# Cross-attention with MLP: context turned by VectorE from 32x32 blocks, a third buffer for the exponentials, new orders

## What is computed

```python
qn = layer_norm(Q, ln_q_g, ln_q_b)                     # Q: [16, 512, 256]
q = heads(qn @ Wq + bq)                                # 16 heads of 16
k, v = heads(KV @ Wk + bk), heads(KV @ Wv + bv)        # KV: [16, 1601, 256]
attn = softmax(einsum('bhqd,bhkd->bhqk', q, k) / sqrt(16))
ctx = einsum('bhqk,bhkd->bhqd', attn, v)
x = Q + (merge(ctx) @ Wo + bo)
h = layer_norm(x, ln_ff_g, ln_ff_b)
return x + silu(h @ W1 + b1) @ W2 + b2
```

## Time and profile before

| | us |
|---|---|
| median of 3 runs | 3438.5 (3438.05 to 3440.09) |
| the profiled execution | 3438.9 |
| its span, first to last instruction | 3437.1 |

### The profile page before, as it was taken

The page is one execution under the profiler, slowest core; times in us unless marked ns, Lnnn a source line. Parts: engine busy times, 40 slices in busy tenths (PEclk is TensorE's granted clock), DMA queues, the critical chain, the costliest instruction groups (busy, mean ns, idle before and its releaser), DMA issues.

```text
span 3437.1 us, 52453 instructions
## 1 busy us (share of the span) xinstructions
PE 3363.7 (98%) x19620; PEld 1621.4 (47%) x19620; DVE 2505.0 (73%) x4613; ACT 2240.1 (65%) x2859; POOL 952.1 (28%) x1340
## 2 busy tenths in 40 slices
PE   6899999999999999999999999999999999999997
PEld 2334544444444445444445444444444455444435
DVE  5777777777777867777777777767777777777761
ACT  2566667666676666667666676666767666676663
POOL 5032324223332322324222232232314222242201
PEclk7999999999999999999999999999999999999998
DMA  4322212232122322212232122321223231122200
GB/s 103 64 42 44 51 33 55 45 71 42 35 48 36 71 45 43 50 37 57 45 69 38 32 54 38 70 45 35 51 39 61 45 64 36 35 55 43 45 7 13
DMA packets 121534, 162.95 MB, mean 47 GB/s; under 512 B 37040, under 2 KB 102592, under 8 KB 118208
## 3 DMA queue, kind: packets, MB, share of 16 engines
q1 hardware_dynamic: 120896, 159.40, 23.6%
q10 hardware_dynamic: 384, 0.20, 0.0%
HBM read 46.43 MB, written 8.39 MB: 16 GB/s over the span
## 4 chain that ended last, share of the span: by engine, by line
PE 95%; DVE 2%; ACT 1%; SPq 0%; DMA 0%; issue 0%; POOL 0%; ACTq 0%; DVEq 0%
PE o_ps L1241 23%; PE rows_ps L1207 22%; PE scores L1222 21%; PE side L1171 6%; PE side L1175 6%; PE side L1160 5%; PE side L1152 5%; DVE chunk_max L1006 2%; PE side L1156 2%; PE side L1164 2%; PE side L1143 1%; PE side L1146 0%; ACT probs L811 0%; PE scores L1171 0%; PE side L1167 0%; PE side L1150 0%
## 5 line engine op out<-in xcount | busy, mean ns | idle before, releaser
L1006 DVE TENSOR_REDUCE chunk_max<-rows_ps 128x1 f32<-128x512 f32 (+1 forms) x3328 | 2110.8, 666 | 778.7 <-PE rows_ps L1207 772.0
L811 ACT ACTIVATE probs<-scores 128x1024 f32<-128x1024 f32 (+1 forms) x1664 | 1653.4, 1022 | 727.8 <-PE scores L1222 559.7
L1207 PE MATMUL rows_ps<-k_stack,q_stack 96*128 96x512 bf16 (+1 forms) x4096 | 1139.5, 337 | 22.6 <-DVE chunk_max L1006 15.9
L1222 PE MATMUL scores<-q_stack,k_stack 99*128 99x512 bf16 (+1 forms) x3328 | 984.9, 379 | 5.0 <-ACT probs L811 3.0
L1241 PE MATMUL o_ps<-probs,v_sb 128*32 128x512 f32 x6656 | 850.2, 602 | 2.3 <-ACT probs L811 2.2
L1207 PEld LDWEIGHTS rows_ps<-k_stack,q_stack 96*128 96x128 bf16 x4096 | 338.3, 98 | 717.7 <-DVE chunk_max L1006 469.7
L1222 PEld LDWEIGHTS scores<-q_stack,k_stack 99*128 99x128 bf16 (+1 forms) x3328 | 320.0, 99 | 391.1 <-issue 94.5
L1241 PEld LDWEIGHTS o_ps<-probs,v_sb 128*32 128x32 f32 x6656 | 148.9, 108 | 359.8 <-issue 280.9
L648 POOL TENSOR_TENSOR o_sb<-o_sb,denom 128x512 f32<-128x512 f32 x32 | 40.6, 1268 | 896.5 <-DVE denom L992 896.5
L592 POOL TENSOR_TENSOR rest<-whole,k_parts 128x512 f32<-128x512 f32 x124 | 117.1, 944 | 548.7 <-ACT k_parts L776 541.8
L1175 PE MATMUL side<-w_sb,ffT 128*128 128x256 f32 x960 | 261.3, 381 | 0.0
(11 more groups left out here) (130 smaller groups left out, 2160.0 us busy)
## 6 DMA issues: line engine op xcount, KB each, us to landing
k_stack<-k_parts SPq DMA_DIRECT2D x768, 50.0 KB, 2.2
k_stack<-k_stack SPq DMA_DIRECT2D x192, 200.1 KB, 5.6
ctx_nat<-in_ctx SPq DMA_DIRECT2D x47, 512.0 KB, 4.0
q_stack<-q_stack SPq DMA_DIRECT2D x192, 64.0 KB, 3.4
q_stack<-q_parts SPq DMA_DIRECT2D x756, 16.0 KB, 1.8
x_nat<-in_x SPq DMA_DIRECT2D x16, 512.0 KB, 6.0
resid<-in_x SPq DMA_DIRECT2D x32, 256.0 KB, 2.8
out<-resid SPq DMA_DIRECT2D x32, 256.0 KB, 2.4
```

The source lines that it names most:

```text
L811: nc.scalar.activation(probs[0:rows, (q + t) % 2, 2 * LQ * pair:2 * LQ * (pair + 1)], scores[0:rows, 2 * LQ * pair:2 * LQ * (pair + 1)], A ...
L1006: nc.vector.tensor_reduce(dst, src, AX.X, ALU.max).then_inc(rows_read, 1)
L1207: last = nc.tensor.matmul(rows_ps[:, m % 2, d0:d0 + w], q_stack[s][0:STACK, h, P * t:P * (t + 1)], k_stack[s][0:STACK, h, k0:k0 + w], star ...
L1222: ins = nc.tensor.matmul(scores[0:keys_in(t), LQ * j:LQ * (j + 1)], k_stack[s][:, h, P * t:P * t + keys_in(t)], q_stack[s][:, h, :], start ...
```

## The change

Context is no longer transposed by PE. SP loads it so that each 32 x 32 block of (keys, channels) lies where its transpose has to be, and DVE turns all blocks of a [128 x 512] tile with one `transpose`. A DMA can't move blocks between partition groups and keep one simple pattern, so each chunk takes 8 DMAs (4 groups of 32 partitions x 2 halves of the channels), whose contiguous runs are 32 floats = 128 bytes; the last chunk takes 8 more for its one left key. Chunks 2 and 3 are loaded once DVE has turned chunks 0 and 1. A tile of chunks 0 to 2 is one transpose of 128 x 512, one of chunk 3 is 128 x 96; 8 per batch, letter `t` in `VECTOR[1]`. The 8 `ctx` steps leave PE's and ACT's lists (26 letters `d`, 8 letters `r` of quarter 1). `probs` gets a third buffer: the exponentials of tile t wait for tile t-3. The three order strings are new for all quarters.

```diff
+BLOCK = 32
+BLOCKS = (LK + BLOCK - 1) // BLOCK
+PROBS = 3
 BOTH = (
...
-    [("ctx", (c, kc)) for c in range(2) for kc in range(KC)] + [("w1", (0, 3))]
-    + [("ctx", (c, kc)) for c in (2, 3) for kc in range(KC)] + [("k", (0, c)) for c in range(4)]
+    [("w1", (0, 3))] + [("k", (0, c)) for c in range(4)]
     + [("x", 0), ("x", 1), ("q", 0), ("turn", 0), ("w2", (0, 0))],
 TENSOR = (
-    "pmddsssmmsddddddmssmpmdsssdmdsmddsdddmmpssmmsddmdmdssspmmsddddmddssddmpmmdssssmdmpmmssssmddddmpmsmds"
-    "mdmssddmsmppmsmdssmdmssmdmdmssmsspdmmssdddmssssmddddmppmmddsssmsdmdmpmm",
-    "sspmddmddssmsmddddsmssmpmddddmssssmddddmpssssmmddddmmssssmddmddppmddddmssmssmdpdmmssdmssmdsmmppmmdsm"
-    "dsmmsssdmdssmmpddmmssssddddmmpmddddmssssmmddppmddddmssssmdmddmdmssssmdmdddmmp",
-    "psmmsssddmmddsmdsdmmddssssmmppmdsmsddssmmdddddmssssmmddddppmdmddddddmdsmsssmddddmmpmdddmssmdssdmddms"
-    "dmsssmpmmsspsmmsssdmdmsddmmpsddmsmspssmssmddssmmpdsdddmmpmdmsssmdmpmmss",
-    "dssmmpmsssmsdmmpmsddssmsmdddmmdpmmssssdmmdmssmssmppmssmdssmmssdmdmsdssmmppmmsdsmdmsdmssmddmssmddmdmp"
-    "pmmdssssdmmddssmddmssspddmmspmsssdsdmddmpmssmssmpmm",
+    "pmmssssmddmdddssmmdddssssmmddddssmddmsddmsssmdmddmdmpppmssmsdsmdddmssmdddmsdmsssmddmpmmpmddddmsmsssm"
+    "ddmmddsmsssmppsmmddsmddmsmsssmddddsmmsppdmmdddssssmdmdmssmdmssmsdsmmppp",
+    "ssdssmmddmssmssmpmssmssmpmmsssspmdssssmmpppmsssmsmdssmmssdmssmssmdmmppmmssdmssmssmmdmdmmpmddsmssdddd"
+    "mmpmddddsssmmdmdmmppsmddddsmssmddmdmddmdmsssmsddmmp",
+    "pmmdssmdmssdmsmsdddmmssddmsmsssddmdmdddddmmssssddmdmdpppsmmsssdddmdmdddsdmmsssdmdmsddsmmppmmdssmssmd"
+    "ddmssmddddmmsssdmsmdddmmppddmmssddmmsspppdmdddssmssmdmmssssmdssmmppmmss",
+    "dmsmsssmdsmmpmddmsssmdmdsmsdmdmsssmsmdmdsmmppmmsssdmdmdssdmmpppmmdsssmsdmdmssmdssmdmsdmdmsssdmmpppmm"
+    "ssssdmdmsdmdsdssmmdddssssmmpmdddsmsssmpmdmssssmpmmp",
 VECTOR = (
-    "mmmimimmmmmmmmmmabmmbbmmmmmmmmmmmmmmammbmmmmmmmmnmmgmbmmbgmmmmmmmg",
-    "mmmmmmimmmmxmmxmmimmxmmmmmmmmmmmmmmmmmmmmmmmmgnmmmmmmmmmmmmy",
+    "mmmmimmimmmmmmmmambbbmmmmmmmmmmmmmmmmmabmmmmmbmmmgnmmmmmmmmmmgbmmg",
+    "xmmmmxmmmmttmimmittmmmxmmgmmmmmmmttmmmmmmmtmtmmmmmmmmmnmmmmmmmmmmmmmy",
...
-PROLOGUE = ([(0, "ctx", (c, kc)) for c in (0, 1) for kc in range(KC)] + [(0, "k", 0), (0, "k", 1)]
-            + [step for c in (2, 3) for step in [(0, "ctx", (c, kc)) for kc in range(KC)] + [(0, "k", c)]]
-            + [(0, "x", 0), (0, "x", 1), (0, "q", 0)] + [(0, "v", c) for c in range(NCH)]
+PROLOGUE = ([(0, "k", c) for c in range(NCH)] + [(0, "x", 0), (0, "x", 1), (0, "q", 0)] + [(0, "v", c) for c in range(NCH)]
...
-        ctx_nat = sb("ctx_nat", [P, 2, 4, D])
-        ctxT = sb("ctxT", [P, KC, LK])
+        ctx_blocks = sb("ctx_blocks", [P, 2, KC, CHUNK])
+        ctxT = sb("ctxT", [P, KC, BLOCK * BLOCKS])
...
-        probs = sb("probs", [P, 2, 4 * LQ])
+        probs = sb("probs", [P, PROBS, 4 * LQ])
...
             def load_ctx(b, c):
...
+                dst, landed, _ = ctx_place(b, c)
+                if b == 0 and c == NCH - 1:
+                    sp.wait_ge(beside_set, 1)
+                elif b > 0:
+
+                    sp.wait_ge(ctx_turned, (b * NCH + c - 1) * KC)
+                first, blocks = CHUNK * c, min(CHUNK // BLOCK, (LK - CHUNK * c) // BLOCK)
+                left = LK - first - BLOCK * blocks if c == NCH - 1 else 0
+                for p in range(P // BLOCK):
+                    for kc in range(KC):
+                        channels = slice(P * kc + BLOCK * p, P * kc + BLOCK * (p + 1))
+                        src = ctx[b, first:first + BLOCK * blocks, channels].rearrange("(j r) i -> r j i", r=BLOCK)
+                        to = dst[BLOCK * p:BLOCK * (p + 1), kc, 0:BLOCK * blocks].rearrange("r (j i) -> r j i", i=BLOCK)
+                        sp.dma_start(to, src).then_inc(landed, 16)
+                        if left:
+                            sp.dma_start(dst[BLOCK * p:BLOCK * p + left, kc, BLOCK * blocks:BLOCK * (blocks + 1)],
+                                         ctx[b, LK - left:LK, channels]).then_inc(landed, 16)
...
                     load_x(b + 1)
                     for c in (2, 3):
 
-                        wait_apart(sp, side_ready, step_value(start, kinds.index(("ctx", (c - 2, KC - 1)))))
                         load_ctx(b + 1, c)
...
-                    wait(act, pv_done, per_quarter(KT, b, q, t - 1))
-                nc.scalar.activation(probs[0:rows, (q + t) % 2, 2 * LQ * pair:2 * LQ * (pair + 1)],
+                    wait(act, pv_done, per_quarter(KT, b, q, t + 1 - PROBS))
+                nc.scalar.activation(probs[0:rows, probs_of(b, q, t), 2 * LQ * pair:2 * LQ * (pair + 1)],
...
+            def turn_ctx(b, n, values_made):
+
+                c, kc = divmod(n, KC)
+                place, landed, loads = ctx_place(b, c)
+                w = BLOCK * ((width(c) + BLOCK - 1) // BLOCK)
+                if kc == 0:
+                    dve.wait_ge(landed, loads)
+                if n == 0 and b > 0:
+
+                    dve.wait_ge(side_ready, values_made)
+                nc.vector.transpose(ctxT[:, kc, CHUNK * c:CHUNK * c + w], place[:, kc, 0:w]).then_inc(ctx_turned, 1)
...
             def prologue():
                 nc.vector.memset(inverse[:, :, :], 0.0)
                 nc.vector.memset(neg_parts[:, :, :, :], 0.0)
+                for n in range(2 * KC):
+                    turn_ctx(0, n, None)
                 for stage in range(STAGES):
                     x_moments(0, stage)
-                for use in range(NCH + 1):
+                split_first(0)
+                for n in range(2 * KC, NCH * KC):
+                    turn_ctx(0, n, None)
+                for use in range(1, NCH + 1):
                     split_first(use)
...
+                    elif what == "t":
+                        if b < B - 1:
+                            before = FIRST[0] if b == 0 else BOTH[0]
+                            turn_ctx(b + 1, next(turn), step_value(start, before.index(("v", (1, NCH - 1))) - len(before)))
...
-                    if kind == "ctx":
...
+                    if kind == "k" and s == 0:
+
+                        pe.wait_ge(ctx_turned, b * (NCH * KC) + (arg + 1) * KC)
```

More of the change, by code:

```diff
@@ L120 @@
+    "xmmmmxmmmmttmimmittmmmxmmgmmmmmmmttmmmmmmmtmtmmmmmmmmmnmmmmmmmmmmmmy",
+    "mmmmmmmmymmmmmmimmmmmmmmmmmmgmmmmmmmmmmmmmminmmmmmmmmmmgmm",
+    "mmmmmmmmmmmmmmmmmgmmmmmmigmmmmmmmmmmyimmmmmmmnmmymmmmmmmmmm",
 )
@@ L167, in products @@
 def products(kind, arg):
-    if kind in ("v", "ctx"):
-        c = arg if kind == "v" else arg[0]
-        return [(t, kc) for t in tiles_in(c) for kc in (range(KC) if kind == "v" else [arg[1]])]
+    if kind == "v":
+        return [(t, kc) for t in tiles_in(arg) for kc in range(KC)]
     first, second = {"turn": (QT, 1), "x": (QT, 1), "k": (1, KC), "q": (1, KC), "wo": (2, 2), "h": (KC, 2), "w1": (2, KC), "w2": (1, FM)}[kind]
@@ L328, in xattn_kernel, with ctx_place @@
         hT_of, ffT_of, h_of = [hT, late_hT], [ffT, late_ff], [h_nat, late_h]
+        def ctx_place(b, c):
+            loads = [16 * KC * (P // BLOCK) * (2 if n == NCH - 1 else 1) for n in range(NCH)]
+            if b == 0 and c >= 2:
+                place = ffT[:, 4 * (c - 2):4 * (c - 2) + 4, :].rearrange("p m q -> p (m q)")
+                return place.rearrange("p (k n) -> p k n", k=KC), ctx_beside[c - 2], loads[c]
+            done = loads[c] if b == 0 else b * (loads[c % 2] + loads[c % 2 + 2]) - loads[c % 2 + 2] \
+                + (loads[c % 2] if c < 2 else loads[c % 2] + loads[c])
+            return ctx_blocks[:, c % 2, :, :], ctx_landed[c % 2], done
         def opening_bank(n):
@@ L351, in xattn_kernel @@
         ones_set = sem("ones_set")
+        beside_set = sem("beside_set")
         stack_ones = sem("stack_ones")
@@ L404, in per_quarter, with probs_of @@
             return b * (4 * n) + (n * q + more)
+        def probs_of(b, q, t):
+            return per_quarter(KT, b, q, t) % PROBS
         def walk(eng, prologue, quarter, epilogue, tallies=()):
@@ L742, in side_step @@
                 act.wait_ge(side_ready, step_value(start, k))
-                if kind == "ctx":
-                    c, kc = arg
-                    last = nc.scalar.copy(ctxT[:, kc, CHUNK * c:CHUNK * c + width(c)], src[:, 0:width(c)])
-                elif kind == "turn":
+                if kind == "turn":
                     last = nc.scalar.copy(shift_parts[:, :], src[0:4 * PARTS, :])
@@ L837, in quarter @@
             def quarter(b, q, start, steps):
-                unit, reads = iter(range(UNITS)), iter(chosen(q, steps, ("v", "ctx", "k", "q", "x", "turn", "h", "w1")))
+                unit, reads = iter(range(UNITS)), iter(chosen(q, steps, ("v", "k", "q", "x", "turn", "h", "w1")))
                 for what in SCALAR[q]:
@@ L1045, in quarter @@
                 bm, qm = (b, q + 1) if q < 3 else (b + 1, 0)
-                row, stage, x_stage = itertools.count(), iter(range(2)), iter(range(STAGES))
```

(18 more changed lines are left out.)

26 lines of the change are left out of this document (7 added, 19 removed).

## The result

The changed kernel takes 3571.5 us (median of 4 runs, 3570.2 to 3574.7), the kernel before 3439.0 beside it: 1.0387 times as long (95% interval 1.0369 to 1.0405), 132 us more. I had said 58 us more, with a range that ends at 3600. The sign and the place were right; the size was less than half of what it is.

What follows compares the result with a forecast made beforehand. PE, 95% of the last chain, was taken as the bound: 3438.9 - 42 (transposes) - 44 (bursts) + 132 (wait for x) + 12 (opening) = 3496.9, say 3497 us, range 3435 to 3600.

Steps and rivals of the forecast that it cites:

- What leaves PE: PE's sequence: 26 transposes, 2.8 us a batch (-42 us), and 12 fewer bursts of p, 2.8 us (-44 us).
- merged bursts give nothing: Rival on PE's bursts of p: PE then waits for exponentials, the -44 is missing, 3541 us; chance 0.07.
- What DVE gets: DVE's quarter 1: turns add 4.6 us, 45 us in 49.0, over 90% full but free if DVE starts on time.
- What SP gets, steps 1 to 4: SP's queue at quarter 1: 16 context issues (8.3 us) delay x, landing at +8.5; DVE waits, maxima behind it.
- Step 5: PE in quarter 1: stands 8.0 us for maxima plus 0.8 of DVE backlog, 8.8 a batch, +132 us.
- Packets of 128 bytes: Context DMA: 16 ns a packet, 8.2 us for 8192 over 16 engines, about the issuing time, so little added.
- The slow-packet rival: Context DMA: 31 ns a packet, x lands at +16, 3609 us; chance 0.15 including a queue that pushes back.
- The opening: Launch start: 36 more issues (18.7 us) precede the first k's last load; +12 us once, bounds +8 to +20.
- "No wait": Rival at quarter 1: x is there when DVE comes or the order hides it, 3365 us; chance 0.13.
- The turning point: Quarter 1: the sign changes where PE's wait is under 5 us a batch, x landing at +5.

Runs made afterwards that it cites:

- the fastest kernel: Changed kernel with x loaded ahead of context, opening loads reordered and DVE's first two x letters later in quarter 1: 3364.0 us, ratio 0.9783.
- the kernels with x first: Changed kernel with x loaded ahead of context chunks 0 and 1: 3376.6 us; with opening reordered too, 3369.9; with DVE's x letters later as well, 3364.0.
- DVE's other order: Changed kernel, loads unchanged, DVE's letters for the moments of x later in quarter 1, behind maxima: 3405.8 us, ratio 0.99.
- the filled stand: Changed kernel, loads unchanged, PE repeating one useless score product 36 times where it stood waiting in quarter 1: 3516.0 us, ratio 1.0225.

## Why the prediction was right and wrong

**What leaves PE: right.** The sum of letters was 5.6 us a batch. The kernel in which nobody waits for x has 207.29 - 201.70 = 5.6. The transposes are 2.8 a batch, as forecast. I counted 42 bursts before and 30 after; the runs of p that meet across the quarters' borders count once, which makes it 41 and 28, one more saved, 0.23 a batch and 3.7 us in all. The rival "merged bursts give nothing" is out: the transposes alone would leave 207.3 - 2.8 = 204.5. The other 2.8 belong to the bursts by this subtraction and by the 0.23 us of a burst; no run has the third buffer without the new strings, or the old strings with it. One thing in this term was wrong: I multiplied the bursts by 16, but the last batch has no gain (from the last `turn` but four to the last 195.6 us, before 195.4). With the opening as it is after, the kernel without a wait would take 3364.0 + 6.6 = 3370.6 us where I had 3365: that is most of the 7 us that the clock leaves.

**What DVE gets: right.** A whole turn takes 0.68 us and a short one 0.27, estimated at 0.70 and 0.2. Once x is there, they are free.

**What SP gets, steps 1 to 4: right.** Issues of 0.525 us (0.52 forecast), the first of them 2.9 us before the quarter (3.7), x issued 5.55 us into the quarter (4.6), landed 4.1 later (4.0), and DVE at the first letter `x` waits with all maxima behind it, 158.7 us in 16 batches where I wrote some 9 us, 15 times.

**Step 5 is the one that failed: the size of a stand.** It has 8.0 us of stand and 0.8 of backlog, 8.8 a batch. The stands of PE are 7.8 to 10.3 us by its starts, 9.4 on average, and 0.8 of that is there in the fastest kernel too. So the wait is 8.6, against 8.8: right in sum. The backlog isn't in it, since the period adds up without one; x came 1.1 us later than the +8.5 at the border shown. What the term leaves out is what PE does *after* the stand: the clock is at half for 13.65 us, from 1662.5 to 1676.2 at the border shown (2.5 us of the window from 1660 and 1.2 of that from 1675), of which PE stands for 4.2 and works for 9.5. Work at half the clock gives 9.5 / 2 = 4.7 us lost, and 8.6 + 4.7 = 13.3 is the whole of 215.0 - 201.7. Against 8.8 the term was too small by 4.5 a batch, 67 us: the loads were said to cost 132 us and cost 13.3 x 15 = 200. I had read a clock of 1.00 in the earlier trace rows and carried it into a period that had been given a hole of 8 us. The Trainium skill (TensorE: Matmul & The Clock Gate, Part 1: The HAM clock gate) says that half clock is the state of an idle engine, and that activity lifts it. The trace of the kernel after agrees: 0.50 in 15 of 15 batches, each time at a stand of 7.8 to 10.3 us. I hadn't weighed it in this step.

**Packets of 128 bytes: right, as cheap.** This is the queue while the 16 issues move their 8192 packets, from 1652.37 to 1662.5 us (packets, MB, share of 16 engines):

```profile
q1 hardware_dynamic: 8495, 1.09, 69.8%
```

16 x 10.13 x 0.698 / 8495 is 13 ns a packet, where I had 16. Two chunks are 8192 x 13 / 16 = 6.7 us of each engine, less than the 8.4 of the issuing, so nobody waits for it. The slow-packet rival needed x to land at +16; it landed at +9.6. A byte costs twice what it did in packets of 1 KB, which take some 51 ns: the queue carries 307552 packets on 25.1% of the engines' time, where the page before has 120896 packets on 23.6%, 84 us of each engine more (896 - 811) for the same bytes. The Trainium skill (DMA: Bandwidth & Descriptors, Specifications) asks for at least 512 bytes for line rate. The traces agree that the rate is lower below it, 13 ns for 128 bytes and 51 for 1 KB; that had no price in the time of this kernel.

**The opening: 12.1 us for 12, by luck in part.** The first product of k starts 12.2 us later (25.07 and 12.87). The issues ahead of it take 15.5 us more and not 18.7, since those of the last chunk are shorter; the last load lands 2.2 us after its issue where it took 5.4, 3.2 sooner and not 2; and the 4 us that turned context was to save didn't come, for from there to the first shift it is 82.0 us after and 82.1 before. The errors cancel. What the first k waits for was right, but it isn't the only gate: with that wait gone, v waits for the last load.

**The rivals.** "No wait" said 3365 us, and the kernels with x first measured 3364 to 3377: right for the kernel that the change could have been. The turning point that I gave for the sign, a wait of 5 us, was too high: with four issues ahead of x the stands are 1.9 to 5.2 us, 3.3 on average, and the kernel is already 0.6% slower than before.

What stays open is what decides whether a short stand lowers the clock. Its length alone doesn't: the kernel with x behind four issues has 2.79 us without and 2.30 with a fall, and by starts there is a stand of 3.2 us without one (DVE's other order) and one of 1.6 with one (the filled stand).

## What to carry to other kernels

When a queue gets more issues, recount every item behind them at the measured pitch (16 x 0.525 us here), and look at what the engine that waits for the last one has standing behind its wait. A stand of PE must be priced twice: its length, and then half of the time that PE works while the granted clock is at half, 1.6 to 5.9 us a stand here. The second part doesn't shrink in step with the stand, so halving a wait gives back much less than half. If a wait can't be removed, another order that keeps the engine at work is worth most of it (166 of 195 us here).

## What the hardware showed that I had not expected

- The granted clock fell to 0.5 in all 15 batches with stands of 7.8 to 10.3 us, in all 15 with 3.7 to 6.6 us, in 12 of 15 with 1.9 to 5.2, for 6.8 to 13.7 us. A fall costs half of what PE works in it: 4.3 to 5.0 us behind the long stands, 3.4 to 5.9 behind the middle ones, 3.4 to 5.1 behind the short ones. Taking four us of nine off the stand gave back 56 of 195 us.
- Useless matmuls in the place of a stand made the kernel 55 us faster, without any transfer landing earlier.
- Context in packets of 128 bytes took each DMA engine 84 us more of a span of 3568, 13 ns a packet, and the kernels with x first carry them too and are 1.8 to 2.2% faster than the kernel before.
